# A one-hot expert product on 64x64 tiles of the TensorE array in place of 64x128

## What is computed

```python
sim = einsum('pbnhd,hkpd->pbnhk', q, keys)       # 8 heads, two halves p, 32 keys each
sx, ix = top_k(sim[0], 8); sy, iy = top_k(sim[1], 8)
scores, pk = top_k(all_sums_of(sx, sy), 8)       # 8 of 64 pairs
indices = take(ix * 32 + iy, pk)                 # expert id, 0 .. 1023
h = gelu(einsum('bnd,bnhkd->bnhk', x, down_embed[indices]))
out = einsum('bnhk,bnhkd->bnd', softmax(scores) * h, up_embed[indices])
```

## Time and profile before

| | |
|---|---|
| median of 3 runs | 3595.06 us (3592.42 to 3595.2) |
| profiled execution | 3593.08 us, its span 3591.3 us |
| expert loop (30 passes) | 2112.9 to 3144.9 us of the span |
| mean granted TensorE clock | 0.856 of full speed |

### The profile page before, as it was taken

How to read it: one execution, slowest core, us unless ns; L and a number is a source line. 1 busy time by engine, 2 the same in 40 slices (tenths; PEclk the granted TensorE clock), 3 DMA queues, 4 the chain that set the end, 5 groups by cost and what they waited for, 6 DMA issues and landing times. The chain is left out here.

```text
span 3591.3 us, 82463 instructions
## 1 busy us (share of the span) xinstructions
PE 3069.3 (85%) x32284; PEld 2455.2 (68%) x32284; DVE 2606.2 (73%) x8488; ACT 1313.8 (37%) x2231; POOL 184.3 (5%) x155
## 2 busy tenths in 40 slices
PE   5999999999999999999999568778888887763555
PEld 2888888888888888888888535555656555551222
DVE  4565766756657667566565579999999999946775
ACT  2544454454545545445454122222222222211222
POOL 0000000000000000000000000000000000002220
PEclk9999999999999999999999856766666666666777
DMA  1000000000000000000000110000000000000000
GB/s 64 1 1 7 1 1 7 1 2 7 1 7 1 1 8 1 1 7 1 7 1 1 45 48 0 0 0 0 0 0 0 0 0 0 0 10 7 12 12 18
DMA packets 6415, 25.26 MB, mean 7 GB/s; under 512 B 1360, under 2 KB 1872, under 8 KB 5840
## 3 DMA queue, kind: packets, MB, share of 16 engines
q1 hardware_dynamic: 6224, 22.57, 1.6%
HBM read 14.18 MB, written 8.39 MB: 6 GB/s over the span
## 5 line engine op out<-in xcount | busy, mean ns | idle before, releaser
L605 PEld LDWEIGHTS obank<-v_one,probs 128*128 128x128 f32 x8192 | 1069.2, 190 | 91.1 <-issue 2.6
L605 PE MATMUL obank<-v_one,probs 128*128 128x129 f32 x8192 | 1078.6, 274 | 0.0
L352 ACT ACTIVATE probs<-bank 128x512 f32<-128x512 f32 x1024 | 583.8, 597 | 746.9 <-PE bank L593 450.9
L442 DVE TENSOR_REDUCE maxes<-ring 128x1 f32<-128x512 f32 x1024 | 659.5, 686 | 129.0 <-PE ring L573 105.7
L592 PE MATMUL bank<-q_hh,k_hl 128*128 128x512 f32 x1024 | 505.2, 493 | 1.1 <-issue 0.7
L593 PE MATMUL bank<-q_lm,k_h 65*128 65x512 f32 x1024 | 406.6, 397 | 0.0
L455 DVE RECIPROCAL recip<-obank 128x1 f32<-128x1 f32 x512 | 83.4, 163 | 414.5 <-PE obank L605 401.2
L573 PE MATMUL ring<-k_hl,q_hh 128*128 128x512 f32 x1024 | 338.4, 410 | 10.4 <-DVE k_hl L434 6.0
L1054 PE MATMUL ring<-up,z 128*128 128x128 f32 x1024 | 175.7, 352 | 128.5 <-DVE parts L971 127.1
L965 DVE TENSOR_TENSOR low_hot<-ids,low_iota 128x16384 f16<-128x16384 f16 x32 | 278.1, 8692 | 9.1 <-ACT ids L865 6.0
L1054 PEld LDWEIGHTS ring<-up,z 128*128 128x128 f32 x1024 | 170.5, 265 | 140.2 <-issue 138.7
(11 more groups left out here) (220 smaller groups left out, 3499.2 us busy)
## 6 DMA issues: line engine op xcount, KB each, us to landing
xt<-in_x SPq DMA_DIRECT2D x8, 512.0 KB, 8.3
out_x<-xt SPq DMA_DIRECT2D x8, 512.0 KB, 2.6
x<-out_x SPq DMA_DIRECT2D x1, 4096.0 KB, 12.1
out_x<-x SPq DMA_DIRECT2D x8, 512.0 KB, 2.6
pk_wq<-in_w_q SPq DMA_DIRECT2D x1, 1024.0 KB, 4.9
pk_wqT<-in_w_qT SPq DMA_DIRECT2D x1, 1024.0 KB, 7.1
wmod_sb<-in_wmod SPq DMA_DIRECT2D x2, 384.0 KB
w_qk_sb<-in_w_qk SPq DMA_DIRECT2D x1, 512.0 KB, 4.3
```

The source lines that it names most:

```text
L352: nc.scalar.activation(probs[:, half, i, :], st[s % 4], ACT.Exp).then_inc(st_free[s % 4], 1)
L442: nc.vector.tensor_reduce(maxes[:, i, k:k + 1], ring[bank_of(at)][:], AX.X, ALU.max).then_inc(rows_maxed, 1)
L605: mm = nc.tensor.matmul(obank[j % 2][:, 0:D + 1], probs[:, half, m, cols], v_one[h % 2][:, m, :], start=(m == 0), stop=(m == TB - 1))
```

## The change

An expert id (0 to 1023) is split as high = id >> 6 (16 values) and low = id & 63, in place of id >> 7 and id & 127. `low_hot` becomes 64 wide, `high_hot` and `value_hot` 16 wide. The highs lie in `high_iota` (and so in the columns of `value_hot`) with the even ones first and then the odd ones. For each token, part and tile there are now two products with the same 64x64 stationary operand: columns 0 to 7 (even highs) go to PSUM partitions 0 to 63, columns 8 to 15 (odd highs) to partitions 64 to 127. What lies in PSUM afterwards is what lay there before, so that `weigh` and `combine` are unchanged. `expert_weights` has 1024 products in place of 512. One semaphore increment (`products_begun`) stands between the waits and the products.

```diff
-            nc.scalar.activation(low_iota[:], count[:], ACT.Copy).then_inc(consts_made, 1)
-            nc.scalar.activation(high_iota[:], count[:, 0:8], ACT.Copy).then_inc(consts_made, 1)
+            nc.scalar.activation(low_iota[:], count[:, 0:LOWS], ACT.Copy).then_inc(consts_made, 1)
+            nc.scalar.activation(high_iota[:].rearrange("p (j e) -> p e j", j=2), count[:, 0:16].rearrange("p (e j) -> p e j", j=2), ACT.Copy).then_inc(consts_made, 1)
...
-        low_hot = sb("low_hot", [P, P, P], F16)
+        low_hot = sb("low_hot", [P, P, LOWS], F16)
...
-        high_hot = sb("high_hot", [P, P, 8], F16)
-        value_hot = sb("value_hot", [P, P, 2, 8], F16)
+        high_hot = sb("high_hot", [P, P, 16], F16)
+        value_hot = sb("value_hot", [P, P, 2, 16], F16)
...
-                nc.vector.tensor_scalar(chosen_u[:, 1, :], chosen_u[:, 0, :], 127, None, ALU.bitwise_and).then_inc(steps, 1)
+                nc.vector.tensor_scalar(chosen_u[:, 1, :], chosen_u[:, 0, :], LOWS - 1, None, ALU.bitwise_and).then_inc(steps, 1)
...
-                nc.vector.tensor_scalar(chosen_u[:, 2, :], chosen_u[:, 0, :], 7, None, ALU.logical_shift_right).then_inc(split_ready, 1)
+                nc.vector.tensor_scalar(chosen_u[:, 2, :], chosen_u[:, 0, :], 6, None, ALU.logical_shift_right).then_inc(split_ready, 1)
...
+                nc.tensor.sem_inc(products_begun, 1)
                 for t in range(P):
                     for part in range(2):
                         for q in range(2):
                             rows = slice(64 * q, 64 * q + 64)
-                            mm = nc.tensor.matmul(wide[q][:, 8 * t:8 * t + 8], low_hot[rows, t, :], value_hot[rows, t, part, :],
-                                                  start=(part == 0), stop=(part == 1))
+                            for odd in range(2):
+                                mm = nc.tensor.matmul(wide[q][64 * odd:64 * odd + 64, 8 * t:8 * t + 8], low_hot[rows, t, :], value_hot[rows, t, part, 8 * odd:8 * odd + 8],
+                                                      start=(part == 0), stop=(part == 1))
```

More of the change, by code:

```diff
@@ L767 @@
 SLOTS = 20
+LOWS = 64
 W_SCALE = 32768.0
@@ L810, in build_experts @@
         apart = sem("ex_apart")
+        products_begun = sem("ex_products_begun")
         steps = sem("ex_steps")
@@ L964, in one_hots @@
                 dve.wait_ge(ids_ready, u + 1)
-                nc.vector.tensor_tensor(low_hot[:].rearrange("p t (m j) -> p t m j", j=2), spread(ids[:, 0], 2, P // 2),
+                nc.vector.tensor_tensor(low_hot[:].rearrange("p t (m j) -> p t m j", j=2), spread(ids[:, 0], 2, LOWS // 2),
                                         spread(low_iota[:].rearrange("p (m j) -> p m j", j=2), 1, P), ALU.is_equal).then_inc(hots_ready, 1)
-                nc.vector.tensor_tensor(high_hot[:].rearrange("p t (m j) -> p t m j", j=2), spread(ids[:, 1], 2, 4),
+                nc.vector.tensor_tensor(high_hot[:].rearrange("p t (m j) -> p t m j", j=2), spread(ids[:, 1], 2, 8),
                                         spread(high_iota[:].rearrange("p (m j) -> p m j", j=2), 1, P), ALU.is_equal).then_inc(steps, 1)
@@ L975, in one_hots @@
                     last = nc.vector.tensor_tensor(value_hot[:, :, part, :].rearrange("p t (m j) -> p t m j", j=2),
-                                                   high_hot[:].rearrange("p t (m j) -> p t m j", j=2), spread(parts[:, part], 2, 4), ALU.mult)
+                                                   high_hot[:].rearrange("p t (m j) -> p t m j", j=2), spread(parts[:, part], 2, 8), ALU.mult)
                 last.then_inc(hots_ready, 1)
@@ L1473, in build @@
             count = ex("count", [P, P])
-            low_iota = ex("low_iota", [P, P], F16)
-            high_iota = ex("high_iota", [P, 8], F16)
+            low_iota = ex("low_iota", [P, LOWS], F16)
+            high_iota = ex("high_iota", [P, 16], F16)
             slot_iota = ex("slot_iota", [P, SLOTS, P], F16)
```

## The result

The changed kernel takes 4160.38 us in the median (4159.31 to 4161.9, 4 runs) against 3595.13 us; the ratio is 1.157 with a 95% interval of 1.155 to 1.159. The forecast was 4057 us with a range of 3780 to 4325. The mechanism that was forecast is there; its size was 103 us too small.

A forecast was written before the change was run, and what follows sets the result against it. VectorE bounds the kernel now; refetched code was to make TensorE the bound at 49.2 us a pass. Loop +444 us, with the ends together +462, gave 4055 on the profiled execution and 4057 in the median, range 3780 to 4325.

The forecast's parts named there:

- VectorE's saving: Expert loop: low_hot -4.3 us, high_hot +0.5, value_hot +1.1; net -2.7 us a pass, worth nothing in the loop.
- The limit: TensorE's loop code: 4.5 blocks stay, 12.9 do not; 8.5 blocks assumed wholly refetched every pass.
- The sum: Whole kernel: loop +444 us, before it -2.7, behind it +9.4, -5.2 and +16.2; together +462 us.
- Behind the loop: TensorE after the loop: expert_weights(30) to last turn +9.4 us, turn to expert_weights(31) -5.2, then to last combine +16.2.
- Ahead of it: Before the expert loop: value_hot(0) is on the path and comes 2.7 us sooner.
- Turn to combine: TensorE's pass: turn 0.9 us and activations 6.8 us, both at their old price.
- no wait for `parts`: TensorE's pass: parts comes 6.6 us after the turn, activations end 6.8 or more after it, so the wait goes.
- front: TensorE's pass, from the end of expert_weights to the next turn: 10.0 us, less 1.04 us of wait already taken off.
- Stays at today's price: Rival: loop body stays on the core, products 13.1 ns each, pass 36.4 us, total about 3690 us; chance 0.10.
- partly fetched: Rival: only blocks that don't fit are fetched, two or three 1.6 us stops, about 3790 us; chance 0.06.
- Serial loads: Rival: weight loads one after another, 1024 x 51 ns = 52 us, pass 75 us, up to 4880 us; chance 0.07.
- side-by-side rival: Body stays, column halves overlap, expert_weights about 6.6 us (decides under about 9.8), total about 3543 us; chance 0.05.

The follow-up runs named there:

- one part: Changed kernel with the products of only the first f16 weight part on TensorE, VectorE still building both: 3508.29 us.
- wide kernel: Kernel before (64x128 weights) with the first part's product issued three times, 1024 products a pass and about 2183 instructions: 4314.22 us.
- 1832: Changed kernel with the products of 106 of the 128 tokens of a tile, 848 products: 3949.89 us.
- 2024 instructions: Changed kernel with the products of 118 of the 128 tokens of a tile, 944 products: 4060.82 us.
- 102-token: Changed kernel with the products of 102 of the 128 tokens of a tile, 816 products: 3527.26 us.
- half-and-half kernel: Whole computation, tokens 0 to 63 in the changed 64/16 split, 64 to 127 in the old 128/8 split: 3584.09 us, ratio 0.9975 to the kernel before.

## Why the prediction was right, and where its size was off

*VectorE's saving* was right to a few hundredths: `low_hot` takes 4.426 us (said 4.4), and the pass that VectorE sets is 31.5 us where the code stays (one part: 2608.64 to 2640.15). The saving is worth nothing in the changed kernel, as said (VectorE waits 21.2 us a pass, (298.9 + 294.5) / 28), and some 75 to 77 us where the code stays.

*The code's length decides*: shown from both sides. The wide kernel with as many instructions has the same stops, the narrow kernel with few has none, and 4 per cent of the products make 423 us.

*The limit* was the step that held by luck. The rows of before leave every limit open between the 4.5 blocks that stay and the 12.9 that do not; that 8.5 would not stay was my estimate, and no row shows it. The first expectations put the limit at 8 blocks, 2048 instructions: the highest whole number that the two kernels leave open, and not shown by a run either. The runs show that 7 blocks stay and 8 do not (with 1832 and with 2024 instructions, fewer than 2048, the whole body came anew, 9 packets a pass). The forecast needed only that 9 blocks do not fit, and so it survived. That a block fetched ahead takes the eighth place fits the one packet too many in each pass; it was argued from the counts and not tested by itself. A limit of 7 blocks for any other reason would give the same runs. And in attention four stretches of one pass each (549 to 1516 us) bring 15 to 17 packets where matmuls and loads alone fill 12.9 blocks; how long that body is was not counted.

*The sum* was 462 us and the span grew by 568 (3591.3 to 4159.2). Behind the loop I had +20.4 and it is +20.4 (446.4 us before from 3144.89 to the end, 466.8 now from 3692.43). Ahead of it I had -2.7 and it is -1.6. The miss lies in the pass: 49.2 forecast, 52.7 measured (2111.37 to 3692.43, 30 passes), and 30 x 3.5 is the 105 us. By term, in the pass shown above (53.0 us; the terms together are 3.8 us over the forecast):

- expert_weights 29.3 in place of 26.2. I took the shortest distance between blocks, 3.47 us from the first pass of before; in the changed kernel it is mostly 3.75 with some of 4.02. And there are eight distances (the first of 2.8 us) and not seven with a full last block of 1.9, since the last three products lie in a ninth block. This term alone is 3.1 us a pass.
- A stop of 2.0 us between combine and the first product, which I had set at zero. I covered the fetch behind the branch with a combine of 5.3 us; combine runs in 3.8 now, so that together they are 5.78 us from its start to the products, 0.5 more than forecast. In the wide kernel, where combine takes 5.7, the stop is 1.1 us.
- Combine is faster because of the clock: granted 1.00 in the changed kernel (2528.3 to 2532.0), where in the pass of before it was 0.50 from 2522.7 to 2525.0 and 0.85 on the mean of the next 3 us. The same 3.81 us stand in the one-part and the 102-token kernels, whose combine runs at 1.00 too. In the changed kernel the clock was 0.50 through front and turn and rose during activations (0.94 on the mean of 2523.5 to 2526.1); why it rises sooner than before is not shown. I had held the other work at its old price.
- Turn to combine 7.6 us as said (0.9 + 6.8 against 2520.66 to 2528.25), but 2.1 of them are a wait for `parts`, because activations run faster (4.9 us), by the same rise of the clock. My "no wait for `parts`" was wrong, at no cost to the sum.
- front 10.35 in place of 10.0 (2563.29 to 2573.64). I had taken 1.04 us off as a wait for VectorE's `to_turn`. They stand ahead of the turn in the changed kernel too, as "issue", although VectorE has written `to_turn` by 2551.3. It is ScalarE that fills them: its copy of the last similarities (L851, 0.60 us from 2572.64) and behind it its copy of the ids into `to_turn` (L862, 2573.13 to 2573.54), which the turn at 2573.64 waits for. In the kernel before the same two copies lie there (2510.43, and 2510.92 to 2511.33, ahead of the turn at 2511.43). What did go is half of the wait for ScalarE's first copy inside front, from 1.20 to 0.55 us.

*The rivals.* "Stays at today's price" and "partly fetched" have fallen. "Serial loads" has fallen most clearly: a narrow product costs 8.3 ns at the full clock and 13.3 at the lower one, not 51. The 51 was an estimate: half of the 102 ns of the earlier trace rows for half of the columns, and no row shows that it halves.

The side-by-side rival was half right about the array. Four narrow products take the place of two wide ones; at the full clock they need 33 ns against 25, less than double, and at the lower clock 53 against 26, the double. Whether the halves overlap at the full clock or a narrow product is shorter by itself, no run shows. Its bound of 9.8 us does not follow from the sum either: 31.5 less the 23.0 of the other work is 8.5. With 102 tokens 816 products take 8.5 us, and the 208 missing would come at the lower clock: 2.8 us more, 11.2 for all. TensorE waits in that kernel, on the mean of 19 passes (2200 to 2800 us), 1.95 us before its similarities and 0.27 before combine. So had the body stayed, TensorE would have become the bound by about 0.6 us a pass, and the change would have been some 30 us faster than before. This is an estimate: the 67 us of the 102-token kernel, less two more blocks of 3.5 us in each of three passes with new code, less 30 x 0.6.

## What to carry to other kernels

Count the instructions of a written-out loop body on the engine that runs it before doubling it, and look at the transfers of the instruction queues in the loop: in every run here no packets in the loop (bodies of up to 1768 instructions) went with no "issue" stops among the products, and the next block (1832 instructions) made every pass fetch all of it. Here that step was worth 423 us for 4 per cent more work, which is more than the 84 to 121 us that the fastest versions here won even by leaving work out. Cheap short instructions in great number are the dangerous kind, since 256 of them ran in 1.2 to 1.9 us and a new block took 3.5 to 4; long ones hide the same fetch, as in the attention loop, where TensorE is busy for 240.07 of 242 us with 17 packets. And compare the price of short products at equal granted clock: two prices from one pass can stand on two sides of a change of the clock.

## What was unexpected

- 7 blocks of 16 KB stay in TensorE's loop and 8 do not: about 1768 instructions 3527 us, about 1832 instructions 3950 us.
- The distance between fetched blocks is not one number: 3.47, 3.75 and 4.02 us alternate in the same loop with no other transfers. It does not follow TensorE's clock: the block at 3696.25 runs in 1.19 us at a granted 1.00, the next one in 1.88 at 0.50, and it comes 3.74 us later all the same. What sets it is open.
- What a product costs hangs on the clock for one form and hardly for the other, both with 8 moving columns: 64x64 8.3 ns at a granted 1.00 and 13.3 at 0.50 (102 tokens), 64x128 12.5 and 13.2 (kernel before). In one pass of the half-and-half kernel the 512 narrow ones take 8.5 ns each and the 256 wide ones 13.3, but the narrow ones run at 1.00 throughout and the clock falls to 0.50 within the wide ones.
